# Token and router normalisations of the middle batches scaled by ScalarE instead of VectorE, and the router rows' transposes moved to the next turn

## What is computed

```python
h = tok(x, ccm, ccm_bias, shifts, slopes, conv_w, conv_b)     # image to 256 tokens of 256 values
h = concatenate([h, txt], axis=1)                             # 384 tokens
a = layernorm(h)                                              # (a - mean) / sqrt(var + 1e-5)
c_kv = a @ W_DKV; k = c_kv @ W_UK; v = c_kv @ W_UV; q = a @ W_UQ   # 16 heads of 16
probs = softmax(where(causal, q @ k.T / 4, -inf))
h = h + (probs @ v) @ W_O
xf = layernorm(h)
weights, experts = top_k(softmax(xf @ router_w), 2)
# each choice: the first 384 tokens of an expert (in token order): gelu(x @ w1[e]) @ w2[e], times the weight
h = h + moe(xf) + bias
```

## Time and profile before

| | us |
|---|---|
| median of 3 runs | 653.29 |
| lowest, highest | 652.76, 656.85 |
| profiled execution | 657.03 |
| its span | 655.3 |
| PE busy in the span | 591.5 (90%) |
| DVE busy | 403.9 (62%) |
| ACT busy | 366.8 (56%) |
| POOL busy | 400.6 (61%) |

### The profile page before, as it was taken

The page is one execution under the profiler, slowest core; times in us unless marked ns, Lnnn a source line. Parts: engine busy times, 40 slices in busy tenths (PEclk is TensorE's granted clock), DMA queues, the critical chain, the costliest instruction groups (busy, mean ns, idle before and its releaser), DMA issues.

```text
span 655.3 us, 13051 instructions
## 1 busy us (share of the span) xinstructions
PE 591.5 (90%) x4712; PEld 489.4 (75%) x4712; DVE 403.9 (62%) x955; ACT 366.8 (56%) x817; POOL 400.6 (61%) x618
## 2 busy tenths in 40 slices
PE   2677899999899998989998999999999999999992
PEld 2344556666656666666574999999999999999992
DVE  5789788888998888687662463333444445443220
ACT  5347786777777675665631545454454545454540
POOL 6503243425556545556746799998888887887223
PEclk9889999999999999998898899999999999999997
DMA  7637666633534242471103645454444434452113
GB/s 259 161 82 187 200 203 173 197 104 100 146 100 115 65 111 68 121 229 35 51 32 96 214 138 113 113 112 113 113 114 113 100 82 83 102 113 44 23 21 36
DMA packets 67729, 75.09 MB, mean 115 GB/s; under 512 B 7224, under 2 KB 62242, under 8 KB 67664
## 3 DMA queue, kind: packets, MB, share of 16 engines
q1 hardware_dynamic: 56384, 60.73, 31.0%
q0 software_dynamic: 9504, 13.00, 11.5%
q10 hardware_dynamic: 1776, 0.51, 0.3%
HBM read 31.62 MB, written 22.48 MB: 83 GB/s over the span
## 4 chain that ended last, share of the span: by engine, by line
PE 63%; DVE 11%; ACT 9%; issue 6%; POOL 3%; DMA 3%; SPq 3%; ACTq 1%; POOLq 0%; DVEq 0%
PE t_bank L1872 21%; PE bank L1887 14%; PE s_bank L1887 7%; PE bank L736 4%; DVE mx L1254 3%; PE t_bank L795 3%; ACT part L1087 2%; SPq L417 2%; ACT pt L1031 2%; PE t_bank L702 2%; PE s_bank L1857 2%; PE t_bank L779 1%; DVE wr L1316 1%; PE bank L830 1%; ACT pt L1029 1%
## 5 line engine op out<-in xcount | busy, mean ns | idle before, releaser
L1832 DVE TENSOR_TENSOR hl<-h,hh 128x384 fp32r<-128x384 f32 x128 | 100.4, 789 | 156.4 <-ACT h L1795 156.3
L582 POOL TENSOR_SCALAR_AFFINE_SELECT pt<-pt 128x256 f32<-128x256 f32 x192 | 83.6, 444 | 140.2 <-ACT pt L1031 111.9
L1792 ACT ACTIVATE hh<-t_bank 128x384 fp32r<-128x384 f32 x128 | 63.0, 492 | 135.2 <-PE t_bank L1872 132.9
L1254 DVE TENSOR_REDUCE mx<-s_bank 128x2 f32<-128x256 f32 (+2 forms) x192 | 122.3, 682 | 25.9 <-PE s_bank L682 25.3
L1743 POOL DMA_INDIRECT out<-yo,xr x48 | 74.9, 1561 | 55.2 <-ACT yo L1803 44.8
L1730 POOL TENSOR_TENSOR wl<-wr,wh 128x256 fp32r<-128x256 f32 x112 | 96.9, 900 | 1.2
L1031 ACT ACTIVATE pt<-t_bank 128x512 f32<-128x512 f32 x128 | 75.6, 604 | 29.6 <-PE t_bank L702 28.3
L1872 PE MATMUL t_bank<-xh,wh 128*128 128x384 f32 x256 | 86.9, 340 | 1.0 <-issue 1.0
L1872 PE MATMUL t_bank<-xl,wh 128*128 128x384 f32 x256 | 86.6, 338 | 0.0
L1872 PE MATMUL t_bank<-xh,wl 128*128 128x384 f32 x256 | 86.4, 338 | 0.0
L702 PE MATMUL t_bank<-qs,ks 98*128 98x384 bf16 (+2 forms) x384 | 74.9, 277 | 4.6 <-ACT pt L1031 2.7
(11 more groups left out here) (215 smaller groups left out, 1330.2 us busy)
## 6 DMA issues: line engine op xcount, KB each, us to landing
wr<-in_w SPq DMA_DIRECT2D x16, 1024.0 KB, 5.5
qs<-part SPq DMA_DIRECT2D x96, 96.0 KB
ks<-part SPq DMA_DIRECT2D x90, 96.0 KB
slot_rows<-empty SPq DMA_DIRECT2D x4, 1560.0 KB, 9.5
xr<-slot_rows SPq DMA_DIRECT2D x16, 390.0 KB, 3.3
wr<-in_x SPq DMA_DIRECT2D x7, 768.0 KB, 5.3
out<-hid SPq DMA_DIRECT2D x8, 384.0 KB
qs<-mT ACTq DMA_DIRECT2D x62, 3.0 KB
```

The source lines that it names most:

```text
L582: pool.affine_select(out=blocks, in_=blocks, compare_op=ALU.is_ge, fill=0.0, base=0, pattern=[[0, 2], [1, P]], channel_multiplier=-1).then ...
L1254: ins = dve.tensor_reduce(mx[:, p // 2, 2 * (p % 2):2 * (p % 2) + 2, j], pair_region(s_bank, j), AX_X, ALU.max)
L1792: act.activation(hh[:, f, :], h_banks[f % NH], ACT.Gelu_apprx_tanh)
L1832: dve.tensor_tensor(hl[:, f, :], h[f % 2][:, :], hh[:, f, :].bitcast(F32), ALU.subtract).then_inc(hl_done, 1)
```

## The change

For batches 2 to 7 the first norm's scaling, and for batches 0 to 5 the second norm's, move from VectorE to ScalarE, as one activation per tile: Identity(rstd * h + lift), with lift = -mean * rstd. GpSimd makes `fall` = -mean and `lift` = fall * rstd behind rstd, in `rstds` and `rstds2`. ScalarE scales one tile behind each of the three exponentials of step 3: even turns the tokens of batch b+2, odd turns the rows of batch b-1 (before on VectorE in even step 3 and odd step 2). VectorE keeps the copy of the token's number (`tag`, odd step 2), with a semaphore of its own; `row_done` now counts 3 and not 4 a batch. The transposes of the rows (`rows_back`) and ScalarE's copies of them move from odd step 3 to step 0 of the even turn that follows: the first group directly behind the transpose of the maxima, the second before the values' product. Batches 0 and 1 of the first norm and batches 6 and 7 of the second stay as they were.

```diff
@@ gpsimd: rstds (rstds2 the same way for b < B - 2, with fall2, lift2, lifted2)
             pool.tensor_tensor(rstd[:, :], ve[:, :], neg_half[:, :], ALU.pow).then_inc(rstd_done, 1)
+            if b >= EARLY:
+                pool.tensor_scalar(fall[:, :], mv[:, :, 0], -1.0, None, ALU.mult).then_inc(lifted, 1)
+                pool.wait_ge(rstd_done, b + 1)
+                pool.wait_ge(lifted, 2 * (b - EARLY) + 1)
+                pool.tensor_tensor(lift[:, :], fall[:, :], rstd[:, :], ALU.mult).then_inc(lifted, 1)
@@ tensor
+                if not odd and p == 0 and live(b - 2):
+                    rows_back(b - 2, 0)
...
-                    if odd and live(b - 1):
-                        rows_back(b - 1, 0)
...
-                if odd and p == 3 and live(b - 1):
-                    rows_back(b - 1, 1)
+                if not odd and p == 0 and live(b - 2):
+                    rows_back(b - 2, 1)
@@ scalar
+        def scaled(b, t):
+            if t == 0:
+                act.wait_ge(lifted, 2 * (b - EARLY) + 2)
+                act.wait_ge(xnT_ps, KC * b)
+            act.activation(xn[:, t, :], hid[:, b, t, :], ACT.Identity, bias=lift[:, t:t + 1],
+                           scale=rstd[:, t:t + 1]).then_inc(xn_done, 1)
+
+        def scaled2(b, t):
+            q = b % NROW
+            if t == 0:
+                act.wait_ge(lifted2, 2 * b + 2)
+                if b >= NROW:
+                    act.wait_ge(sent[q], 16 * NT * TOPK * (b // NROW))
+            act.activation(row[q][:, t, 0:DIM], hid[:, b, t, :], ACT.Identity, bias=lift2[:, t:t + 1],
+                           scale=rstd2[:, t:t + 1]).then_inc(row_done, 1)
...
                 if cur:
                     exps(n, p, 0)
+                if odd and p == 3 and live(b - 1):
+                    scaled2(b - 1, 0)
+                if not odd and p == 3 and live(b + 2):
+                    scaled(b + 2, 0)
...
-                if odd and p == 3 and live(b - 1):
-                    rows_back(b - 1, 0)
+                if not odd and p == 0 and live(b - 2):
+                    rows_back(b - 2, 0)
@@ vector
+        def tag(b):
+            q = b % NROW
+            if b >= NROW:
+                dve.wait_ge(sent[q], 16 * NT * TOPK * (b // NROW))
+            dve.tensor_copy(row[q][:, :, DIM:DIM + 1].bitcast(I32),
+                            token[:, NT * b:NT * b + NT].rearrange("p (t o) -> p t o", o=1)).then_inc(row_tag, 1)
...
                     if p == 2 and live(b - 1):
-                        scaled2(b - 1)
+                        tag(b - 1)
...
-                    if p == 3 and live(b + 2):
-                        scaled(b + 2)
```

More of the change, by code:

```diff
@@ L211, in front @@
     rstd = buf("rstd", [P, NT])
+    fall = buf("fall", [P, NT])
+    lift = buf("lift", [P, NT])
     ckvT = buf("ckvT", [P, T], F32R)
@@ L232, in front @@
     rstd2 = buf("rstd2", [P, NT])
+    fall2 = buf("fall2", [P, NT])
+    lift2 = buf("lift2", [P, NT])
     row = [buf(f"row{q}", [P, NT, ROW]) for q in range(NROW)]
@@ L335, in front @@
     row_done = sem("row_done")
+    row_tag = sem("row_tag")
+    lifted = sem("lifted")
+    lifted2 = sem("lifted2")
     rowT_ps = sem("rowT_ps")
@@ L559, in rstds2 @@
             pool.tensor_tensor(rstd2[:, :], ve2[:, :], neg_half[:, :], ALU.pow).then_inc(rstd2_done, 1)
+            if b < B - 2:
+                pool.tensor_scalar(fall2[:, :], mv2[:, :, 0], -1.0, None, ALU.mult).then_inc(lifted2, 1)
+                pool.wait_ge(rstd2_done, b + 1)
+                pool.wait_ge(lifted2, 2 * b + 1)
+                pool.tensor_tensor(lift2[:, :], fall2[:, :], rstd2[:, :], ALU.mult).then_inc(lifted2, 1)
         def residual(b, t):
-            pool.wait_ge(row_done, (NT + 1) * b + NT + 1)
+            pool.wait_ge(row_done, NT * b + NT)
             pool.tensor_tensor(hid[:, b, t, :], hid[:, b, t, :], bias, ALU.add).then_inc(res_done, 1)
@@ L1156, in scalar @@
                     exps(n, p, 1)
+                if odd and p == 3 and live(b - 1):
+                    scaled2(b - 1, 1)
+                if not odd and p == 3 and live(b + 2):
+                    scaled(b + 2, 1)
                 if p == 0 and cur:
@@ L1182, in scalar @@
                     exps(n, p, 2)
+                if odd and p == 3 and live(b - 1):
+                    scaled2(b - 1, 2)
+                if not odd and p == 3 and live(b + 2):
+                    scaled(b + 2, 2)
                 if odd and p == 0 and late(b + 2):
@@ L1384, in scaled2 @@
                                   ALU.subtract, ALU.mult).then_inc(row_done, 1)
-            dve.tensor_copy(row[q][:, :, DIM:DIM + 1].bitcast(I32),
-                            token[:, NT * b:NT * b + NT].rearrange("p (t o) -> p t o", o=1)).then_inc(row_done, 1)
+            tag(b)
         def keep_logits(b):
```

6 lines of the change are left out of this document (3 added, 3 removed).

## The result

The changed kernel takes 678.25 us (median of 4 runs, 676.84 to 680.85); the kernel before took 653.61 on the same chip (4 runs, 652.76 to 656.85). The ratio is 1.0393, with a 95% interval of 1.0351 to 1.0434: slower. The medians lie 24.6 us apart (their quotient is 1.0377, within that interval), where the prediction said 15.6 and a range up to 674. The same kernel on another chip gave 1.0411 [1.0357, 1.0465].

A forecast was written before the change was run, and what follows sets the result against it. No engine was full; a chain of hand-overs bound each 37.5 us batch, and ScalarE's queue would bind after the change. Terms 6.1 + 8.1 + 1.4 = 15.6 us on the median 653.29 gave 668.9, range 652 to 674.

The forecast's parts named there:

- rival A: Attention batches: ScalarE's queue and the bank of the maxima become the bound; 660 to 676 us; chance 0.66.
- Rival B: Even turn: VectorE's 1.15 us leaves the chain in six batches, ScalarE's free time takes the tiles; 646.4 us; chance 0.12.
- Stretches of about 40 us: Sign that the forecast is right: attention batch stretches take about 40 us instead of 37.5.
- Price of a tile: One scaling on ScalarE: 0.57 us duration, 0.48 per tile after overlap; bounds 0.26 to 0.59.
- The lower bound of 0.26: Lowest price of a ScalarE scaling tile: the form without pointer operand (394 ns) less the overlap of about 0.1.
- `fall`: GpSimd's times -1 behind rstd: taken as 0.4 us, bounds 0.2 and 0.8; `lift` ready at 209.65.
- Term 1: Step 3, six batches: ScalarE's token scaling waits for `lift`; 4 x 0.73 + 1.05 + 2.1 = 6.1 us, bounds 0 to 10.
- Term 2: Even step 0: row transposes wait for the maxima's copy; 1.35 us in each of six turns, 8.1; bounds 0 to 9.
- Term 3: Odd step 3: two copies and an idle go, three tiles come on ScalarE; +0.32 four times, 1.4 us; bounds -2 to 3.
- The base: Forecast sum added to the median 653.29 us, not to the profiled execution of 657.03, 3.7 above it.
- The range: 8 in 10: 652 (leaving out the faster rival) to 674 us, with the terms at 8.5, 9 and 3.

The follow-up runs named there:

- xn_only: Against the kernel before: only the tokens' scalings move to ScalarE, the rows' scalings and transposes stay as before; 665.6 us, ratio 1.0171.
- rows_only_filled: Against the kernel before: only the rows' scalings and transposes move, with twelve small matmuls in the wait for the maxima's copy; 660.55 us, ratio 1.0116.
- back_only: Against the kernel before: only the rows' transposes and their copies move to even step 0, both scalings stay on VectorE; 658.61 us, ratio 1.0087.
- filled: Against the changed kernel: twelve small matmuls added on TensorE in the wait before the first row transposes; 677.36 us, ratio 1.0339 to the kernel before.
- rows_latest: Against the changed kernel: first row-transpose group behind step 0's query-key block, second behind the values' product; 679.2 us, ratio 1.0315 to the kernel before.
- the second trace: The changed kernel unchanged, run once more on another chip; 685.26 us, ratio 1.0411 to the kernel before.
- behind_filled: Against the changed kernel: first token tile behind the query-key piece, plus twelve small matmuls in the rows' wait; 669.92 us, ratio 1.0200 to the kernel before.
- after_behind: Against the changed kernel: first token tile moved behind the query-key piece; 677.82 us, ratio 1.0329 to the kernel before.
- behind_latest: Against the changed kernel: first token tile behind the query-key piece, both row-transpose groups late in step 0; 672.67 us, ratio 1.0204 to the kernel before.
- latest_behind_filled: Against the changed kernel: first token tile behind the piece, both row groups late, twelve small matmuls behind the maxima's transpose; 667.4 us, ratio 1.0209.

## Why the prediction was right in direction and wrong in size

- **The direction and its mechanism held.** ScalarE's queue is the bound (rival A), not VectorE's share. Rival B (faster) fell on the row that the prediction named against it: ScalarE's turn comes before `lift`. Stretches of about 40 us were forecast; between the colours of turns 4, 6 and 8 lie 40.50 and 40.71.
- **Price of a tile: right.** 0.50 from start to start (0.48 forecast), 595 ns of duration (0.57). The rows' tile takes 635. (The lower bound of 0.26 is not what its working gives, 394 ns less 0.1, which is 0.29; only the lower bounds use it.)
- **`fall`: 0.4 was too high, the lower bound right.** The six of the first norm take 230 to 252 ns. `lift` came 1.46 after `rstd` began to run (1.55 forecast). Those of the second norm take up to 0.71. GpSimd's timeline in turn 3, and VectorE's at the same time:

```profile
116.82 0.64 POOL L573 TENSOR_SCALAR fall<-mv 128x3 f32<-128x3 f32 x1
```

```profile
116.62 1.41 DVE L1349 SCALAR_TENSOR_TENSOR g<-wr,prm,g 128x512 f32<-128x512 f32 x2
```

A VectorE operation with two inputs in SBUF was running, as beside the 804 ns row. Where VectorE reduces from PSUM the same operation takes 0.23. By the rule of the Trainium skill (SBUF — State Buffer, section "SBUF: two separate sides") on the shared port pair, a VectorE operation with two inputs in SBUF keeps out a GpSimd one that reads SBUF; the trace agrees at both places.
- **Term 1 (the tokens, 6.1 us) is the step that failed first.** It followed ScalarE's queue and asked when the next colour would start (+1.72). From the first exponential of step 3 to the colour it is 6.38 us now and was 3.88: +2.50. It didn't ask which TensorE instruction needs the bank that the delayed piece sets free. The projection does: 1.79 us of wait, which came back to ScalarE as 0.80 before the third exponential. In turns 4, 6 and 8 the part cost 1.80, 1.53 and 1.52, not 0.73; over turns 2 to 10 it was 7.8 against 4.0. Turn 0 was sized right: 1.9 in after and 1.9 to 2.2 in the other kernels with this part, against 2.1 forecast, and within 0.15 of nothing in those without it. Alone (xn_only) it cost 1.7%, some 11 us, with the clock's falls; with the piece in front 0.54%, 3.5 us.
- **Term 2 (the rows' transposes, 8.1) and Term 3 (1.4) were right in the sum, and partly for another reason.** rows_only_filled, without falls of the clock, costs 1.16%, 7.6 us, against 9.5 forecast. In the trace of after the two take 1.2 to 1.8 a turn without a fall (1.35 + 0.32 forecast). The place was right, too: a wait for the maxima's copy. Its forecast length (about 1.0, from the transpose's end at 193.46 to 194.49) is that of back_only, 0.87 to 1.04; with the row tiles ahead of the copy it is 1.51. The cost divides otherwise than the terms did. Rows' part in each turn, us more than before, with no fall of the clock in it up to turn 12 (turn 14 lies where before has falls of its own):

  | turn | 4 | 6 | 8 | 10 | 12 | 14 |
  |---|---|---|---|---|---|---|
  | back_only: transposes moved, no tile on ScalarE | 0.82 | 0.81 | 0.82 | 0.82 | 0.25 | 1.08 |
  | rows_only_filled: with the tiles | 1.82 | 1.49 | 1.39 | 1.39 | 1.26 | 1.22 |
  | filled: with the token part too | 1.80 | 1.48 | 1.62 | 1.39 | 1.23 | 1.22 |
  | rows_latest: transposes behind the key block | 1.68 | 1.36 | 1.50 | 1.25 | 1.11 | 1.28 |

  By the terms the move alone, less what ScalarE gains in odd step 3, was 1.35 - 1.12 = 0.23 a turn, and the three tiles 1.44. Measured are 0.8 in four of six turns for the move, and 0.6 to 1.0 more for the tiles up to turn 12: the move was put too low, the tiles too high, and the errors cancelled. Of the bank's wait little can be won: rows_latest has no wait ahead of the transposes up to turn 12, and its rows' part is 0.11 to 0.14 shorter than that of filled there; its own falls come behind the router's wait, outside this part. That the 0.8 is TensorE's own time for the two groups (2 x 0.38) fits in size; no run tests it.
- **The missing term: TensorE's clock.** The prediction counted a wait by its length. Behind waits of 1.2 to 1.8 us that before didn't have (no wait of TensorE there is over 0.93 from 76 to 293 us), the granted clock falls to 1.2 GHz for a stretch, and the matmuls behind take up to twice as long: +1.5 to 1.7 us a time in the rows' part (3.0 once, in turn 8 of the second trace), +1.7 at the projection (3.58 against 1.89). Two turns of the first trace are hit, 10 and 14, and four of the second (4, 8, 10 and 12, where the rows' part costs 2.8 to 4.7). In the rows' half alone it makes 1.1%, some 7 us (1.0222 against 1.0116). The two halves without falls, 3.5 us (tokens behind the piece) and 7.6 (rows, filled), make 11; behind_filled, which is both, costs 2.0%, 13 us; the whole change costs 24.6. The piece behind the wait and the clock are the other half.
- **The base.** The sum was put on the median, with a profiled execution 3.7 above it. That was right to do: by the traces alone the change is 19.6, by the medians 24.6.
- **The range** ended at 674 because each term's upper end was left at the length of waits. With 1.5 us more for each of the eleven new TensorE waits (six before row transposes, five before projections) on top of the sum, 668.9, it would have reached 685.

## What to carry to other kernels

When an instruction that may wait is put into an engine's queue, list what each instruction behind it sets free (banks above all) and who needs that first; the wait is paid there. Putting the waiting instruction behind the one copy that frees a bank took two thirds of the token part's cost away here. And price a new wait of the matmul engine not at its length alone, but also with the matmuls behind it at half the clock.

## What the runs showed of the hardware beyond what was expected

- The granted clock fell to the lower level behind a single TensorE wait of 1.5 to 1.8 us, with the engine busy before it. It is no fixed consequence: of eleven waits of 1.2 to 1.8 us in the first trace two were followed by a fall, and in another execution of the same program other turns were hit, behind waits of the same length. In xn_only the same projection waits (1.75 to 1.82) were followed by a fall four times of four, in after never.
- A fall taken away at one place came at another: after_behind lost its token waits and had falls in four turns; behind_latest lost its row waits and stood at 0.91 to 0.95 in three stretches, with falls behind waits of 0.82 and 0.70 us, while back_only's single waits of 0.87 to 1.04 had none behind them. Twelve 128x128 bf16 matmuls in the gap (0.84 us busy) held the clock at 1.00 up to 293 us in filled, behind_filled and rows_only_filled, but not quite in latest_behind_filled (0.96 and 0.97 in two stretches).
- An activation with two pointer operands out of SBUF runs in 595 to 635 ns for 128x256, against 483 with one, which reads PSUM.
